# GpSimd's gather program written out with constant waits, and the widening of the source indices moved to it

## What is computed

```python
xn = _layernorm(x)
x = x + gnn(xn, W1, b1, W2, b2, edges) + mixer(xn[None], W_qk, b_qk, W_v, b_v, gamma, beta)[0]
x = x + ffn(_layernorm(x)[None], mask, wr, br, w1, fb1, w2, fb2)[0]

# gnn: two of these, with relu between
def gcn_conv(x, W, b, src, dst, n):
    h = x @ W
    s, d = concatenate([src, loop]), concatenate([dst, loop])
    deg = segment_sum(ones_like(d), d, n)
    dinv = where(deg > 0, rsqrt(deg), 0.0)
    msg = h[s] * (dinv[s] * dinv[d])[:, None]
    return segment_sum(msg, d, n) + b
```

## Time and profile before

| | us |
|---|---|
| median of 3 runs | 5739.9 (5737.3 to 5745.7) |
| the profiled execution | 5720.8 |
| its span, first to last instruction | 5719.0 |
| first gather layer | about 2510 |
| second gather layer | about 2806 |
| GpSimd busy | 3250.5 (57%) |
| TensorE busy | 2936.6 (51%) |
| VectorE busy | 1904.3 (33%) |
| ScalarE busy | 1214.9 (21%) |
| TensorE clock granted, mean | 0.715 of full speed |

### The profile page before, as it was taken

One profiled execution on the slowest core, in us unless ns is written; L12 is line 12 of the kernel. 1 busy time (PEld: TensorE's weight loads), 2 busy tenths in 40 slices (PEclk: granted clock), 3 DMA queues, 4 the chain that ended last, 5 costly groups with the idle time before them and its releaser, 6 DMA issues.

```text
span 5719.0 us, 69449 instructions
## 1 busy us (share of the span) xinstructions
PE 2936.6 (51%) x16356; PEld 2523.6 (44%) x16357; DVE 1904.3 (33%) x5571; ACT 1214.9 (21%) x2622; POOL 3250.5 (57%) x3443
## 2 busy tenths in 40 slices
PE   6544334444433343443266566656656666666663
PEld 5433333333333333333255455555555555555552
DVE  8433333333333233332133233323333332333336
ACT  3311111111111111110022222222223222322221
POOL 4566666666666666666555555555555555555550
PEclk8766666666666666666587778777778787787776
DMA  3211111111111111111211111111111111111115
GB/s 108 70 45 46 46 46 47 46 46 46 45 46 46 45 46 46 46 46 46 55 45 44 42 43 45 43 42 42 45 45 42 44 45 41 43 44 45 42 42 183
DMA packets 191338, 288.38 MB, mean 50 GB/s; under 512 B 59596, under 2 KB 137588, under 8 KB 191094
## 3 DMA queue, kind: packets, MB, share of 16 engines
q0 software_dynamic: 106496, 218.32, 13.4%
q1 hardware_dynamic: 83572, 68.55, 3.8%
q10 hardware_dynamic: 1232, 1.05, 0.1%
HBM read 249.19 MB, written 38.49 MB: 50 GB/s over the span
## 4 chain that ended last, share of the span: by engine, by line
another core or an unknown queue 34%; issue 19%; PE 16%; DVE 14%; DVEq 11%; ACT 5%; POOL 0%; DMA 0%; ACTq 0%; SPq 0%; POOLq 0%
PE bank L883 6%; PE bank L745 3%; DVEq L329 3%; PE bank L873 3%; DVE arena L1171 2%; DVE acc L1182 2%; ACT arena L616 1%; DVE drel L1162 1%; DVEq L1240 1%; DVEq L1229 1%; DVEq L1162 1%; DVE arena L1027 1%; PE bank L859 1%; DVE arena L1231 1%
## 5 line engine op out<-in xcount | busy, mean ns | idle before, releaser
L493 POOL DMA_INDIRECT arena<-table,idx_now x3328 | 3148.3, 946 | 2202.5 <-DVEq L1193 1110.8
L745 PE MATMUL bank<-arena 128*128 128x128 f32 x6656 | 1108.9, 328 | 625.3 <-issue 397.3
L745 PEld LDWEIGHTS bank<-arena 128*128 128x128 f32 x6656 | 1050.3, 242 | 667.4 <-issue 654.2
L1182 DVE SCALAR_TENSOR_TENSOR acc<-bank,from_base,acc 128x128 f32 x416 | 145.0, 349 | 1601.4 <-remote 1551.7
L774 PE MATMUL bank<-ident,arena 128*128 128x128 f32 x196 | 67.3, 447 | 1145.7 <-ACT arena L586 1130.1
L873 PE MATMUL bank<-arena 128*128 128x128 f32 x3136 | 509.5, 338 | 253.9 <-ACT arena L612 163.1
L1171 DVE TENSOR_TENSOR arena<-bank,drel 128x512 f32<-128x512 f32 x832 | 536.0, 686 | 244.7 <-issue 190.6
L873 PEld LDWEIGHTS bank<-arena 128*128 128x128 f32 x3136 | 490.8, 251 | 277.6 <-ACT arena L612 176.7
L883 PE MATMUL bank<-arena 128*128 128x256 f32 x1568 | 498.9, 479 | 159.6 <-ACT arena L616 109.3
L774 PEld LDWEIGHTS bank<-ident,arena 128*128 128x128 f32 x196 | 28.2, 203 | 1164.5 <-ACT arena L586 1148.6
L883 PEld LDWEIGHTS bank<-arena 128*128 128x128 f32 x1568 | 375.6, 248 | 261.3 <-ACT arena L616 130.4
(11 more groups left out here) (237 smaller groups left out, 3079.6 us busy)
## 6 DMA issues: line engine op xcount, KB each, us to landing
arena<-table,idx_now POOLq DMA_INDIRECT x3328
base_rows<-arena SPq DMA_DIRECT2D x98, 128.0 KB
xs<-in_x_dram SPq DMA_DIRECT2D x6, 1792.0 KB, 16.4
acc<-base_rows SPq DMA_DIRECT2D x9, 896.0 KB, 9.8
out_dram<-acc SPq DMA_DIRECT2D x8, 896.0 KB, 7.7
table<-acc SPq DMA_DIRECT2D x7, 896.0 KB, 4.8
table<-acc SPq DMA_DIRECT2D x98, 64.0 KB
arena<-base_rows SPq DMA_DIRECT2D x5, 896.0 KB, 11.8
```

Of the source, the lines that this page charges most:

```text
L493: pool.indirect_dma_start(ring[:, quarter * HALF + k, :], None, table[layer], bass.IndirectOffsetOnAxis(ap=idx_now[:, i, c:c + 1], axis=0) ...
L745: last = nc.tensor.matmul(visit_sum[h][:, 0:F], S[:, h, k, :], ring[:, quarter * HALF + k, :], start=(k == 0), stop=(k == HALF - 1))
L1182: last = dve.scalar_tensor_tensor(a, visit_sum[h][:, 0:F], mask[:, ds(turn, 1)], a, ALU.mult, ALU.add)
```

## The change

GpSimd's `gather_layer` is no longer a hardware loop. It is written out for all 26 rounds, so that each wait compares with a constant, and the increments of `s_issue` behind the waits are gone. GpSimd widens the indices itself, a round of four pairs in one instruction (64 columns), into one of two sets of `idx_now`. The cast for the next round stands behind the second pair of a round. The first cast of each layer stands ahead of the wait for the layer's table. `s_idx` is now a single semaphore, and GpSimd waits for it once a round. VectorE's `next_indices`, its call in both loops and its two first casts are gone, and so are the spare columns of `src_idx` with their memset.

```diff
-        src_idx = sb("src_idx", [P, CHUNKS + 2 * PAIR], i16)
+        src_idx = sb("src_idx", [P, CHUNKS], i16)
-        idx_now = sb("idx_now", [P, SETS, PAIR], i32)
+        idx_now = sb("idx_now", [P, 2, SETS * PAIR], i32)
...
-            pool.memset(src_idx[:, CHUNKS:CHUNKS + 2 * PAIR], 0).then_inc(s_const, 1)
...
+            sets = PAIRS // SETS
+
+            def next_indices(gg):
+                pool.tensor_copy(idx_now[:, gg % 2, :], src_idx[:, gg * SETS * PAIR:(gg + 1) * SETS * PAIR])\
+                    .then_inc(s_idx, 1)
+
             def gather_layer(layer):
-                with pool.Fori(0, PAIRS // SETS) as gg:
+                for gg in range(sets):
+                    pool.wait_ge(s_idx, layer * sets + gg + 1)
                     for i in range(SETS):
-
-                        pool.wait_ge(s_idx[layer], gg * SETS + (i + 1))
-                        pool.sem_inc(s_issue, 1)
                         for h in range(2):
-
                             pool.wait_ge(s_free[layer], gg * (2 * SETS) + (2 * i + h + 1))
-                            pool.sem_inc(s_issue, 1)
                             quarter = 2 * (i % 2) + h
                             for k in range(HALF):
-                                c = h * HALF + k
+                                c = i * PAIR + h * HALF + k
                                 pool.indirect_dma_start(
                                     ring[:, quarter * HALF + k, :], None, table[layer],
-                                    bass.IndirectOffsetOnAxis(ap=idx_now[:, i, c:c + 1], axis=0),
+                                    bass.IndirectOffsetOnAxis(ap=idx_now[:, gg % 2, c:c + 1], axis=0),
                                 ).then_inc(s_gath[layer][quarter], 16)
-
+                        if i == 1 and gg + 1 < sets:
+                            next_indices(gg + 1)
+
+            pool.wait_ge(s_eTe, 2 * (PAIR // 4))
+            next_indices(0)
             pool.wait_ge(s_tab1, 16 * GROUPS)
             gather_layer(0)
+            next_indices(0)
             pool.wait_ge(s_tab2, 16 * TILES)
             gather_layer(1)
...
-            dve.wait_ge(s_const, 5)
+            dve.wait_ge(s_const, 4)
...
-            dve.tensor_copy(idx_now[:, 0:2, :], src_idx[:, 0:2 * PAIR].rearrange("p (a c) -> p a c", a=2))\
-               .then_inc(s_idx[0], 2)
...
-            def next_indices(layer, g):
-                dve.tensor_copy(idx_now[:, ds((g + 2) % SETS, 1), :].rearrange("p a c -> p (a c)"),
-                                src_idx[:, ds(g * PAIR + 2 * PAIR, PAIR)]).then_inc(s_idx[layer], 1)
...
-                next_indices(0, g)
...
-                next_indices(1, g)
```

4 lines of the change are left out of this document (1 added, 3 removed).

## The result

| | us |
|---|---|
| before, median of 4 runs | 5738.6 (5704.0 to 5745.7) |
| after, median of 4 runs | 5566.9 (5555.6 to 5582.4) |
| ratio, 95% interval | 0.971 (0.968 to 0.974) |
| profiled execution of after, span | 5582.4, 5580.6 |

The change takes 2.9 per cent, 172 us, off. The forecast was 5660, with 5590 as the range's lower end: right in sign, 23 us outside the range, and less than half of the gain. The profiled executions are 138 us apart (5720.8 and 5582.4), since that of before was among the shorter ones and that of after is the longest of its four. One of the ten executions of the changed kernel in a later session (after_again) took 4841.8 us against 4548 to 4560 of the others and counts in no ratio.

What follows compares the result with a forecast made beforehand. GpSimd's row of gathers and the gaps behind it were taken as the bound. Waits -34.5 and -43.5, VectorE's casts -10, GpSimd's casts +5 gave -83, rounded to -80: 5660 us from a median of 5739.9, range 5590 to 5750.

Steps and rivals of the forecast that it cites:

- The bound: First gather layer: nothing but GpSimd's row of gathers, 1571.6 us busy, 484.2 issue idle and 453.6 waiting for the ring.
- The path in the gap: Between pairs, 4.53 us: 3.06 until VectorE sees the sums, 0.61 for two additions, 0.86 to the next gather.
- (a): GpSimd's ring waits: carried by the gather, each costs 0.46 us less; 34.5 us in the first layer, 43.5 in the second.
- Rival B: GpSimd's waits: passed before the gather is handed over, so 0.48 us stays behind; gain 5 to 25 us; chance 0.18.
- C: Rival: held signals come from GpSimd's sequencer, so the first layer's 424 us gap goes, about 5315 us; chance 0.08.
- (d): GpSimd's 52 added casts: 0.2 us each, mostly inside the ring wait; 5 us at most, 31 were the cover gone.
- (e): GpSimd's program grows from 273 to 3520 straight instructions; nothing was taken for it.
- Rival E: GpSimd's straight program waits for 13 to 26 more instruction packets, 31 to 61 us, up to 95; chance 0.07.
- The rule that the prediction set against the change: The skill's engine selection rule leaves elementwise work to VectorE, against moving the casts to GpSimd; no size given.
- I take a quarter off: Second layer's waits: 58 us cut to 43.5, because the feed-forward stage beside the stream doesn't start earlier.
- rival D: Second layer: an earlier stream makes passing second halves wait, 2.7 us each, up to 143 us, about 5800; chance 0.10.
- (c): VectorE loses a cast and two register operations, 0.5 us a pair: first layer nothing, second 10 us of at most 52.

Runs made afterwards that it cites:

- after_again: The changed kernel unaltered, run again beside the kernel before in a later session: 4552.9 us against 4543.0, ratio 1.002.
- after_inc: The changed kernel with the increment of s_issue put back behind each wait for the ring: 5689.7 us, 0.992 of the kernel before.
- waits_only: The kernel before with GpSimd's program written out, constant waits all on gathers, no increments, VectorE still widening: 5588.0 us against 5737.1, 0.977.
- paced8: The changed kernel with all ring waits on gathers, plus each second half's first gather waiting until the first half landed: 5675.6 us against the kernel before's 5788.1, 0.980.

## Why the prediction was off, by its own steps

**Right.** The bound: the first layer is gathers and the gap behind them. The path in the gap: the additions come 3 us after the last gather's end, before and after. The step (a), that the 0.48 us of handing over passes inside the wait once the gather carries it; the Trainium skill's "Perfetto Trace Analysis", section "DMA Instruction — SWDGE (GPSIMD)", has the wait in a queue behind the handing over, and the traces agree: 0.33 us from the additions' end in place of 0.86. The prediction took 0.40, so a wait is worth 0.53 and not 0.46. First layer: 34.5 us forecast, 41 measured, and 75 x 0.53 = 40. The fourth pair keeps the old gap, as said. Rival B is refuted by the 0.33 us, and after_inc brings the 0.86 back; C by the additions that still come 3 us after the last gather.

(d) A cast takes 0.25 us, 0.2 taken, and is hidden inside the wait:

```profile
L482 POOL CAST idx_now<-src_idx x51: 245/250/256, 277.3 to 5279.0; 128x64 int32<-128x64 int16 x51
```

(e) 25 packets more, near the upper end of the 13 to 26 estimated, and no stop that could be seen: "issue" idle time is 0.306 us a gather in the first layer as before. Rival E is refuted. The Trainium skill's "Runtime: NRT & Kernel Launch", section "Instruction fetch mechanics", has blocks of a straight program fetched ahead, and here the trace agrees: between the gathers of a half GpSimd never stands longer than 0.31 us.

The rule that the prediction set against the change doesn't bear on this cast. The Trainium skill's "GPSIMD Engine Reference", section "4.1 Engine selection", has GpSimd slower for elementwise work with two inputs and at roughly line rate with one. The cast has one input; it took 0.25 us, and no run here has the same cast on both engines.

**Wrong: the second layer, by the step "I take a quarter off" and its fixed count of waits.** Forecast were 43.5 us for the waits there, and 96 us is the whole of what this layer lost in the profiles; waits_only lost 109 in its profile without any move of the casts. The quarter was argued from work beside the stream that starts no earlier. The traces show nothing taken off: pairs with two attached waits are shorter by 1.0 us, those with one by 0.4, about 0.53 for each wait. With the shares of before, that is 50 x 1.0 + 50 x 0.4 = 70 us. On top of it 18 pairs in 100 changed kind, from 27.2 to 25.7, another 28 us. Together 98; as both terms come from the two profiles whose layers differ by 96, the sum sorts the difference and doesn't confirm it.

This change of kind is rival D's mechanism with the opposite sign. D said that an earlier stream turns pairs that pass at the second half into pairs that wait there; that happened (116 waits to 164 in the profiles). D priced each at +2.7 us, since the wait stands in the stream. What it left out is that the stand lets held signals through, so that the wait ahead of the next first half is 3.0 us where it is 7.2 behind a pair without a stand. paced8 shows that a stand put in has this effect. The rows for it were there: in one layer, waits of up to 9.5 us and one of 3.54 belonged to the two kinds.

**Too small: (c), the casts.** 10 us were taken out of bounds of 0 and 52, less 5 for (d). Moved alone, the casts give 37 us (18 to 46). Its own profile is 17 us shorter than that of before (4 in the first layer, 16 in the second, 3 longer elsewhere); the other 20 are the distance of the two profiled executions from their medians, and which layer they belong to isn't shown.

With 123 to 135 for the waits and 37 for the casts the sum would have been 160 to 172. The forecast of 80 had 78 and 5.

**Two slips that don't move the forecast.** The prediction took the matmuls from 1521.67 for those whose sums VectorE adds at 1532.43. They are the second half's; the first half's ended at 1520.80, so the delay is 11.6 us and not 8.8. The 3.06 us from the last gather's end, which the sum uses, stay. And in the lower end of the range, 119 us belong to 201 waits (75 in the first layer, 126 in the second), not to 226.

**Not seen: that the hold itself comes and goes.** The trace of before had it in nearly every pair and I took it as given. The 1195 us between 4543 and 5738 are seven times what the change moves, and they decide its sign.

## What to carry to other kernels

A wait that an instruction can carry itself is cheaper than one that stands ahead of it, if what is behind takes long to hand over (here 0.33 us for 0.86): look for semaphore instructions of the sequencer (an increment nobody needs is enough to force one) ahead of DMAs and compare the distance from the releasing event with the distance between two of them. When a kernel has pairs or rounds of two lengths, price a change by how many move from one kind to the other and what each kind lasts, not by the wait that appears in it: the wait may be what makes the kind short. Check such lengths inside rows of one kind, where it doesn't matter where a pair is cut. And where a trace shows signals arriving long after their sender was done, run the same kernel in another session before a sum is built on it.

## What the runs showed of the hardware

In some sessions, while GpSimd issues gathers (128 rows of 512 bytes, one each 1.25 us) in long rows, TensorE's results reach VectorE and ScalarE late, by 11.6 us in the pair of the earlier trace rows and by 13.4 us in the earlier trace rows, and not before some 3 us after the last gather has ended. In the same stretches register instructions of VectorE's and SyncE's sequencers often take 0.7 us in place of 0.04, and matmuls stop for 1.7 to 2.4 us with nothing left to wait for, while signals from ScalarE to TensorE mostly pass within 1 us. Rows of four gathers (5 us) with stands of 2.1 us between them aren't affected, rows of eight (paced8) are in part. In other sessions the results arrive within 0.2 us (0.18 in the row shown) at the same rate of gathers. A fill of 0.13 us that fits between two gathers changes nothing; gaps of 0.8 to 1.1 us help in part. What makes a session one or the other isn't known, nor where the gathers and the other engines meet, nor whether the signals or the engines are what is late.

A wait carried by a gather costs 0.33 us from the end of the freeing instruction, one carried by an instruction ahead of it 0.86. Where a gather waits for the landing of the one before it, it starts 1.8 us behind that one's end when it carries the wait, and 2.3 to 2.4 when the sequencer does.
